# Routed expert rows: transposed by a DMA on ScalarE's queue in place of TensorE and a copy

## What is computed

```python
probs = softmax(x @ gate_w.T)                # 16 experts
vals, idx = top_k(probs, 4)                  # each token goes to 4 experts
w = vals / sum(vals)
act = swiglu(einsum('th,ehi->eti', x, w_gu))     # w_gu: 4-bit codes times scales, 512 -> 2*384
y_e = einsum('eti,eih->eth', act, w_d)           # w_d: 384 -> 512
out = einsum('te,eth->th', combine, y_e)         # plus one shared expert for all tokens
```

## Time and profile before

| | us |
|---|---|
| median of 3 runs | 693.31 |
| lowest, highest | 689.36, 694.84 |
| span of the profiled execution | 689.3 |
| PE busy in it | 622.6 (90%) |
| DVE busy | 496.2 (72%) |
| POOL busy | 327.7 (48%) |
| ACT busy | 325.8 (47%) |

### The profile page before, as it was taken

One profiled execution on the slowest core, in us unless ns is written; L12 is line 12 of the kernel. 1 busy time (PEld: TensorE's weight loads), 2 busy tenths in 40 slices (PEclk: granted clock), 3 DMA queues, 4 the chain that ended last, 5 costly groups with the idle time before them and its releaser, 6 DMA issues.

```text
span 689.3 us, 17258 instructions
## 1 busy us (share of the span) xinstructions
PE 622.6 (90%) x4394; PEld 375.9 (55%) x4395; DVE 496.2 (72%) x1271; ACT 325.8 (47%) x558; POOL 327.7 (48%) x506
## 2 busy tenths in 40 slices
PE   3668869887898999999999999999999999999992
PEld 2444545444554656565555656566565655656550
DVE  5878788989776858588777867688588878867210
ACT  1763577231343554454544455454554545455441
POOL 2521844000235456564646565564655656565432
PEclk9999989998999999999999999999999999999996
DMA  8670111128156875857577684848767587654432
GB/s 235 203 241 1 63 46 70 40 53 276 49 162 152 207 179 118 189 115 189 107 196 174 128 215 82 225 78 204 177 127 186 117 193 174 141 89 68 90 47 31
DMA packets 49841, 93.72 MB, mean 136 GB/s; under 512 B 8840, under 2 KB 16776, under 8 KB 49816
## 3 DMA queue, kind: packets, MB, share of 16 engines
q0 software_dynamic: 16128, 38.35, 30.1%
q1 hardware_dynamic: 32936, 55.04, 27.1%
q10 hardware_dynamic: 752, 0.04, 0.1%
HBM read 65.16 MB, written 28.24 MB: 135 GB/s over the span
## 4 chain that ended last, share of the span: by engine, by line
PE 72%; DVE 13%; ACT 4%; DMA 3%; issue 3%; POOL 2%; SPq 1%; DVEq 0%; POOLq 0%; ACTq 0%
PE gu_ps L1203 41%; PE bank L1231 20%; PE bank L1243 4%; PE bank L1217 4%; DVE mix_room L1023 2%; DMA dn_sc<-dn_scale_halves 2%; DVE act L989 1%; DMA room_a<-in_ctx 1%; ACT acth L620 1%; PE gu_ps L1163 1%; DVE X L998 1%; PE bank L1160 1%; DVE acth L994 1%; DVE dn_code L920 1%; ACT mix_room L579 1%
## 5 line engine op out<-in xcount | busy, mean ns | idle before, releaser
L1203 PE MATMUL gu_ps<-wgu,mix_room 128*128 x1728 | 304.4, 326 | 3.3 <-DVE tick L948 2.1
L1203 PEld LDWEIGHTS gu_ps<-wgu,mix_room 128*128 128x128 f16 x1728 | 166.0, 98 | 114.5 <-issue 7.4
L1231 PE MATMUL bank<-wdn,aT 128*128 (+1 forms) x792 | 186.5, 381 | 4.2 <-ACT aT L627 3.7
L528 POOL DMA_INDIRECT out<-mix_room,idx_s x72 | 123.9, 1721 | 31.9 <-issue 30.5
L627 ACT ACTIVATE aT<-bank 128x768 f16<-128x768 f16 x88 | 71.2, 810 | 130.9 <-PE bank L1217 126.0
L1231 PEld LDWEIGHTS bank<-wdn,aT 128*128 128x128 f16 x792 | 77.6, 98 | 89.5 <-issue 3.2
L989 DVE SCALAR_TENSOR_TENSOR act<-gu_ps,wslot,sg x72 | 44.5, 618 | 96.2 <-ACT sg L613 79.4
L499 POOL TENSOR_TENSOR pool_tick<-ones 128x1 f32<-128x1 f32 x144 | 36.0, 250 | 162.7 <-DMA out<-mix_room,idx_s 79.6
L620 ACT ACTIVATE acth<-act 128x384 f16<-128x384 f32 x88 | 46.0, 523 | 135.8 <-DVE act L989 131.4
L510 POOL DMA_INDIRECT room_b<-token_rows,idx_g x72 | 76.5, 1063 | 12.1 <-issue 3.7
L994 DVE TENSOR_TENSOR acth<-act,acth (+1 forms) x88 | 49.2, 560 | 38.1 <-ACT acth L620 37.6
(11 more groups left out here) (156 smaller groups left out, 586.2 us busy)
## 6 DMA issues: line engine op xcount, KB each, us to landing
dn_sc<-dn_scale_halves SPq DMA_DIRECT2D x34, 384.0 KB
dn_raw<-in_L_ffn_down_packed SPq DMA_DIRECT2D x48, 256.0 KB
gu_sc<-gu_scale_halves SPq DMA_DIRECT2D x34, 192.0 KB
X<-in_x SPq DMA_DIRECT2D x4, 1024.0 KB, 8.1
token_rows<-room_a SPq DMA_DIRECT2D x16, 256.0 KB, 2.3
out<-X SPq DMA_DIRECT2D x4, 1024.0 KB, 10.6
gu_raw<-in_L_ffn_gate_up_packed SPq DMA_DIRECT2D x16, 192.0 KB
gu_raw<-in_L_ffn_gate_up_packed SPq DMA_DIRECT2D x16, 191.9 KB
```

Source lines behind the costliest of these rows:

```text
L528: nc.gpsimd.indirect_dma_start(out[:, :], bass.IndirectOffsetOnAxis(idx_s[:, b:b + 1], 0), y_sb[:, b, :], None, compute_op=ALU.add).then_i ...
L1203: mm = nc.tensor.matmul(ps[b][:, 0:I], x(xp * HC + c), wgu[:, w, wp, c, col:col + I], start=(c == 0 and xp == 0 and wp == 0), stop=(c == H ...
L1231: mm = nc.tensor.matmul(y_ps[0 if shared else b][:, :], aT[:, b, ap, t, :], wdn[:, w, wp, t, :], start=(n == 0), stop=(n == 3 * IC - 1))
```

## The change

PE's `transpose_rows` and ACT's copy of its result are removed. In their place ACT issues one transposing DMA per slot (`dma_start_transpose`, a DMA_TRANSPOSE instruction) from `xg[b]` to `xTs[b]`, 128 partitions x 1,024 f16 values in, 128 x 8 x 128 out. It stands at the head of ACT's slot, ahead of `copy_aT`. Its semaphore `xTs_ld[b]` releases PE's `gate_up(r+1)` and POOL's gather of slot `r+3`.

The DMA takes 128 neighbouring columns at a time, so a row must hold chunk after chunk. `high_x` now writes it so: its two activations read `X` with a step of four and write in order, and `transpose_x` reads 128 neighbouring columns.

```diff
@@ pool: gather
-                    pool.wait_ge(tx_done, s - 1)
+                    pool.wait_ge(xTs_ld[b], 8 * (s - b))
                     pool.wait_ge(wslot_done, s - 1)
@@ scalar: high_x
-                nc.scalar.activation(xhl[:, i % ROWS_AHEAD, 0, :], X[:, i, :], ACT.Identity, scale=xs2[:, i:i + 1],
-                                     bias=xm2[:, i:i + 1]).then_inc(xh_ready, 1)
+                nc.scalar.activation(as_chunks(xhl[:, i % ROWS_AHEAD, 0, :]), by_chunk(X[:, i, :]), ACT.Identity,
+                                     scale=xs2[:, i:i + 1], bias=xm2[:, i:i + 1]).then_inc(xh_ready, 1)
...
@@ scalar: take_rows
                 a.wait_ge(xg_ld[b], 8 * (r - b) + 16)
                 if not isinstance(r, int) or r >= 2:
+                    a.wait_ge(gu_done, NT + r - 1)
+                a.sem_inc(rows_held, 1)
+                a.dma_start_transpose(xTs[:, b, :].rearrange("p (k q) -> p k q", q=P),
+                                      xg[:, b, 0:H].bitcast(F16)).then_inc(xTs_ld[b], 16)
+                a.wait_ge(xg_ld[b], 8 * (r - b) + 16)
+                if not isinstance(r, int) or r >= 2:
                     a.wait_ge(act_done, NT + r - 1)
                 nc.scalar.activation(wslot[:, b, :], xg[:, b, H:ROW], ACT.Copy).then_inc(wslot_done, 1)
-                a.wait_ge(tx_done, r + 1)
-                if not isinstance(r, int) or r >= 2:
-                    a.wait_ge(gu_done, NT + r - 1)
-                nc.scalar.activation(xTs[:, b, :], xT_ps, ACT.Copy).then_inc(xTs_done, 1)
@@ scalar: slot
-                copy_aT(r + (NT - 1), 1 - b)
                 if rows:
                     take_rows(r + 1, 1 - b)
+                copy_aT(r + (NT - 1), 1 - b)
                 activate(NT + r, b)
@@ tensor
-            def transpose_rows(r, b):
-
-                pe.wait_ge(xg_ld[b], 8 * (r - b) + 16)
-                if not isinstance(r, int) or r >= 1:
-                    pe.wait_ge(xTs_done, r)
-                halves = xg[:, b, 0:H].bitcast(F16).rearrange("p (a h) -> p a h", a=2)
-                for k in range(2 * HC):
-                    mm = nc.tensor.transpose(xT_ps[:, k * P:(k + 1) * P], chunk_h(halves[:, k // HC, :], k % HC), id16[:, :])
-                mm.then_inc(tx_done, 1)
...
                 pe.wait_ge(dqg_ready, e + 2)
-                pe.wait_ge(xTs_done, r + 1)
+                pe.wait_ge(xTs_ld[b], 8 * (r - b) + 16)
                 gate_up(s, b, x, w, 0)
                 transpose_act(s - 1, 1 - b)
-                if rows:
-                    transpose_rows(r + 1, 1 - b)
                 gate_up(s, b, x, w, 1)
```

More of the change, by code:

```diff
@@ L286, in gated_xattn_moe @@
         xg_ld = [sem("xg_ld0"), sem("xg_ld1")]
-        tx_done = sem("tx_done")
-        xTs_done = sem("xTs_done")
+        xTs_ld = [sem("xTs_ld0"), sem("xTs_ld1")]
+        rows_held = sem("rows_held")
         wslot_done = sem("wslot_done")
@@ L295, in gated_xattn_moe, with by_chunk, as_chunks @@
         block = ctx.enter_context(nc.Block())
+        def by_chunk(ap):
+            return ap.rearrange("p (q c) -> p c q", c=HC)
         def chunk_h(ap, c):
-            return ap.rearrange("p (q c) -> p c q", c=HC)[:, c, :]
+            return by_chunk(ap)[:, c, :]
+        def as_chunks(ap):
+            return ap.rearrange("p (c q) -> p c q", c=HC)
         def load_expert(sp, gp, dp, buf, n):
@@ L574, in high_x @@
                     a.wait_ge(st_rows[i % ROWS_AHEAD], 16 * (i // ROWS_AHEAD))
-                nc.scalar.activation(xhl[:, i % ROWS_AHEAD, 0, :], X[:, i, :], ACT.Identity, scale=xs2[:, i:i + 1],
-                                     bias=xm2[:, i:i + 1]).then_inc(xh_ready, 1)
+                nc.scalar.activation(as_chunks(xhl[:, i % ROWS_AHEAD, 0, :]), by_chunk(X[:, i, :]), ACT.Identity,
+                                     scale=xs2[:, i:i + 1], bias=xm2[:, i:i + 1]).then_inc(xh_ready, 1)
                 if i >= 2:
                     a.wait_ge(xl_ready, i - 1)
-                nc.scalar.activation(xn[:, i % 2, :], X[:, i, :], ACT.Identity, scale=xs2[:, i:i + 1],
-                                     bias=xm2[:, i:i + 1]).then_inc(xn_ready, 1)
+                nc.scalar.activation(as_chunks(xn[:, i % 2, :]), by_chunk(X[:, i, :]), ACT.Identity,
+                                     scale=xs2[:, i:i + 1], bias=xm2[:, i:i + 1]).then_inc(xn_ready, 1)
             def copy_xT(i):
@@ L1186, in transpose_x @@
                 for k in range(2 * HC):
-                    mm = nc.tensor.transpose(xT_ps[:, k * P:(k + 1) * P], chunk_h(xhl[:, i % ROWS_AHEAD, k // HC, :], k % HC), id16[:, :])
+                    mm = nc.tensor.transpose(xT_ps[:, k * P:(k + 1) * P], as_chunks(xhl[:, i % ROWS_AHEAD, k // HC, :])[:, k % HC, :],
+                                             id16[:, :])
                 mm.then_inc(xT_ps_ready, 1)
@@ L1292, in _ @@
                     route(NT - 1)
-                if i == NT - 1:
-                    pe.wait_ge(route_ready, 1)
-                    transpose_rows(0, 0)
                 shared_gate_up(i, 1)
@@ L1308, in _, with slot @@
             inner = pe.value_load(pairs_i[0:1, 0:1], min_val=E // 2 - 2, max_val=SLOTS // 2 - 2)
-            def slot(r, b, rows=True):
+            def slot(r, b):
                 s = NT + r
@@ L1337, in _ @@
             slot(2 * inner + 2, 0)
-            slot(2 * inner + 3, 1, rows=False)
+            slot(2 * inner + 3, 1)
             transpose_act(2 * inner + 3 + NT, 1)
```

## The result

The changed kernel takes 834.62 us (median of 4 runs, 830.43 to 842.42) against 691.34 us before (689.33 to 694.84): a ratio of 1.208, 95% interval 1.202 to 1.214. Where the runs of a kernel fall into a quicker and a slower group, its ratio is that of the quicker runs. The change is slower by 143 us where 54 were forecast. The direction was right and the time lies inside the range, but it was carried there by another mechanism than the one in the sum.

A forecast was written before the change was run, and what follows sets the result against it. The prediction took PE's back-to-back 6.63 us routed slot as the bound, with DVE partly pacing. A 7.4 us slot added 54 us to the profiled 689.3, giving 743, or 747 us by the median; range 662 to 890 us.

The forecast's parts named there:

- What bounds it, and what is removed: PE's routed slot of 6.63 us falls to 6.18 without transposes; 32 us over 72 slots, about 25 gained.
- The hold on ACT: Issuing the transposing DMA holds ACT's queue, making a slot 7.4 us and adding 54 us over 72 slots.
- the formula: A routed slot takes max(6.18, 3.4 + X) us, from the loops through ACT and PE.
- X: Time the transposing DMA's issue holds ACT's queue per slot: bounded by 0.45 and 8.2 us, taken as 4.0.
- the hold is hidden: Rival: ACT's queue is held at most 2.8 us, the 25 us gain stands, 668 us by the median; chance 0.30.
- The landing: Slot r+1's transposing DMA must land within 5.3 us of issue; costed at nothing at the median.
- The prediction's own rule: With two buffers, a landing beyond 5.3 us costs half of the excess per slot.
- a fall of the granted clock in the waits: Sign on PE: all its terms would grow and the time exceed the forecast; no size given.
- The size of a piece: Each 256 B piece of the transposing DMA takes some 24 ns; 1,024 on 16 engines take 1.55 us.
- The engines as the bound: Rival: DMA engines fill at 91 ns a piece, slot 10.3 us, 960 us; chance 0.15 including holds beyond 6 us.
- What is moved: POOL's gather of slot r+3 waits for the landing instead of PE's transposes; hidden within about 5 us.
- The stride of `high_x`: First-phase activations read with a step of four: left at 0.80 us per tile; doubling would add 26 us of ACT.

The follow-up runs named there:

- its control: The kernel before with the expert weight loads cut to 16 columns each from the fourth weight set on: 685.56 us, ratio 0.9944.

## Why the prediction was right and wrong

**What bounds it, and what is removed: right.** PE's slot went from 6.63 to 6.18 us wherever nothing disturbed it. The 25 us out of 32 were too many. The ticks L974 of the run without weight traffic show 314.66 - 283.25 = 31.4 us for a five-slot expert, against 33.2, which is close to 5 x 6.18 = 30.9. So eight such experts give 8 x 1.8 = 14 us. Between the ticks of four-slot experts there are 26.2 to 26.8 us, and 26.8 to 27.3 in its control, so these give some 0.5 us each instead of 1. That makes 18 us by the ticks and 16 by the addition above.

**The hold on ACT: the formula right, X wrong.** X was bounded by 0.45 and 8.2 us, taken as 4.0, and measured as 1.25. The first step that failed is this choice: it sat on SP's held issue of 3.26 us and on engines 68% busy, and so took the time that the *engines* need for the pieces as time for which the *issuing queue* is held. In these traces the two are apart: the DMA issued at 479.73 us held ACT for 1.25 us and took 14.9 us to land, the one at 437.19 us 1.60 us and 14.84. Nine are held for more than 2 us, 3.82 at most; those beyond 2.8 us stand, like the 2.96 us at 443.16, in a hole in which PE waits anyway. With X below 2.8 the hold is hidden, and the +54 us of the sum are zero. The rival "the hold is hidden" was right in its condition, and its 668 us come near only without the weight loads, 680.1.

**The landing: the second step that failed, and nearly the whole loss.** It was named, its room was worked out (5.3 us), and it was costed at nothing at the median. The median, 4.1 us, bears that out; the time lies in the tail. The bound at hand, 12.1 us for the longest store, was read as a value that every slot might have, not as one that comes back with every expert's loads. The 28 late DMAs took 12.9 us on average. The prediction's own rule, half of the excess over 5.3 us, gives 28 x 7.6 / 2 = 106 us for them, and 125.1 us of waits were measured: the late ones come in pairs that are on their way together, so PE waits once for two. The rule was right; the term was put at nothing. Some 37 us of slower matmuls go with the holes. The prediction named a fall of the granted clock in the waits as a sign, and gave it no price.

**The size of a piece: near, and not enough.** 24 ns was estimated. In a quiet window, 461.0 to 464.6 us, the queues show:

```profile
q10 hardware_dynamic: 1056, 0.26, 38.8%
q0 software_dynamic: 56, 0.15, 22.2%
...
mix_room<-room_b ACTq DMA_TRANSPOSE x1, 3.2
```

That is 0.388 x 3.6 x 16 / 1,056 = 21 ns per piece, landed after 3.2 us. Beside an expert's loads, 480 to 484 us, then 444 to 448 us, and last the loads of the kernel before, beside no transposing DMA, 433 to 437 us there:

```profile
q1 hardware_dynamic: 222, 0.46, 87.2%
q0 software_dynamic: 28, 0.06, 9.9%
q10 hardware_dynamic: 203, 0.04, 8.5%
...
mix_room<-room_b ACTq DMA_TRANSPOSE x1, 14.9
```

```profile
q1 hardware_dynamic: 192, 0.46, 78.3%
q10 hardware_dynamic: 603, 0.15, 36.7%
```

```profile
q1 hardware_dynamic: 423, 0.83, 71.6%
```

In the first of these windows a piece takes 27 ns, and 203 pieces go out against 222 packets of the loads, about one for one. A load packet takes 0.872 x 4 x 16 / 222 = 251 ns. If each of the 1,024 / 16 = 64 pieces of an engine stood behind one such packet, that would be an estimate of 64 x 278 ns = 17.8 us, where 14.9 and 16.4 were measured.

This reading is not shown. No run tested the alternation alone; two transposing DMAs were on their way in that window (issued at 473.17 and 479.73 us); and from 444 to 448 us three pieces go out for each load packet, at 39 ns a piece. It also leaves open why a load packet takes 251 ns there and 261 ns in the second window, where the kernel before has 0.716 x 4 x 16 / 423 = 108 ns (packets of 2.1, 2.4 and 2.0 KB on average). What the windows do show is that the transposes and the loads slow each other. The prediction reckoned the small DMA's share as what the others leave free (32%), and so got 4.8 us; beside the loads that was too little by 4 to 12 us. The mechanism inside the DMA engines stays open.

The Trainium skill, "DMA: Bandwidth & Descriptors", section "Queues, rings and completion order", says that each engine goes round between its queues and drains a packet from one before it turns to the next. The two counts from 480 to 484 us agree with that, as far as the profile's packets are such turns; those from 444 to 448 us would need turns of several pieces. The 9 to 17 descriptors that it gives for a typical packet no run here shows.

**The engines as the bound: not so.** That rival put a piece at 91 ns in every slot. A piece takes 21 to 39 ns in the windows above, and without the loads PE hardly waits. With the loads spread out the same bytes took 104 us less, so the engines are full in stretches, not on the whole.

**What is moved.** POOL's gather waits 204.0 us for landings in 51 places. It was called hidden as long as the landing is within 5 us. Behind the landing of 14.84 us it delayed nothing further: the next DMA was issued at 460.60 us, beside `take_y` at 460.55 us, and landed in 3.2 us. A general cost of these waits is not shown. The stride of `high_x` was left at 0.80 us, the doubling being the upper bound (26 us of ACT, less than half on the path); it measured 1.31 us, and 8.4 us on the path in this kernel, 10.6 alone. The bound was right and the value taken was not.

**Rules weighed ahead.** By the Trainium skill's 1,309 ns per block ("VectorE: DVE Perf Modes", "The three transpose paths", a figure for bf16 where this kernel has f16) the eight blocks one after the other would be an estimate of 10.5 us; a quiet DMA of all eight landed in 3.0 us. The advice for TensorE, which stands in the section "Rules for kernel authors" of that page of the Trainium skill, held in this kernel, for a reason that is not the time of a block. By the Trainium skill, "Advanced Engine Details and Errata", "X-Bar Transpose (TRN2)", transposing DMAs are as fast as plain ones. The trace has 3.0 us at best against 2.0 us for the quickest 256 KB store, so not quite, and beside other traffic far from it.

## What to carry to other kernels

When work goes from an engine to a DMA, ask for its longest landing, not its median, for how many landings are late, and for what else is on the DMA engines at that moment: a wait in a two-buffer loop pays for the tail, and regular bursts such as weight loads make the tail come back on a schedule. Here a transfer in small pieces took some four times as long to land beside loads in packets of 2 KB; the cause within the DMA engines was not isolated. Keep the time that a DMA's issue holds its queue and the time until its data land as two terms, each with its own bound and its own cover.

## What the hardware showed that was not expected

- A transposing DMA of 128 x 1,024 f16 values held the issuing queue for 1.25 us and landed in 3.0 us when the engines were quiet, in up to 16.4 us beside weight loads, with the same bytes. All 28 late landings were the two next behind a set of weight loads.
- The loads suffered as well: a packet of 2.0 KB took 108 ns from 433 to 437 us of the kernel before, and packets of 2.1 and 2.4 KB took 251 and 261 ns in two windows beside transposing DMAs.
- An activation of 128x512 took 0.80 us with f32 read and f16 written in order, 1.31 us with a read step of four, and 2.67 us read in order and written with a step of 128.
- Behind a hole of 9.66 us the granted clock was 0.57 for the next 3.9 us of matmuls, and 1.00 after that.
